# First rows of the q and k stacks loaded from ScalarE's queue, and one value projection moved behind the third attention block

## The reference, cut to what matters

```python
qkv = (xw @ h_qkv_w)                      # window branch: q_w, k_w, v_w
attn = softmax(einsum('bghnd,bghmd->bghnm', q, k) * SCALE)
q = (xh.reshape(B, H * W, C) @ l_q_w)     # pooled branch: 1024 queries
pooled = xh.reshape(B, hg, WS, wg, WS, C).mean(axis=(2, 4)).reshape(B, G, C)
kv = (pooled @ l_kv_w)                    # 256 keys and values
attn = softmax(einsum('bnhd,bmhd->bhnm', q, k) * SCALE)
x = x + attention(_gn(x))
x = x + conv3x3(relu(_gn(x) * mask(_gn(x)))) + bias
```

## Time and profile before

| what | value |
|---|---|
| runs | 347.93, 349.73, 350.08 us (median 349.73) |
| span of the profiled execution | 347.5 us, from its first to its last instruction |
| TensorE busy | 315.2 us |
| VectorE / ScalarE / GpSimd busy | 272.5 / 148.8 / 83.0 us |

### The profile page before, as it was taken

One profiled execution on the slowest core, in us unless ns is written; L12 is line 12 of the kernel. 1 busy time (PEld: TensorE's weight loads), 2 busy tenths in 40 slices (PEclk: granted clock), 3 DMA queues, 4 the chain that ended last, 5 costly groups with the idle time before them and its releaser, 6 DMA issues.

```text
span 347.5 us, 4162 instructions
## 1 busy us (share of the span) xinstructions
PE 315.2 (91%) x1566; PEld 222.3 (64%) x1566; DVE 272.5 (78%) x488; ACT 148.8 (43%) x189; POOL 83.0 (24%) x46
## 2 busy tenths in 40 slices
PE   0879968999979999999799999999799999999995
PEld 0566344267866663688567744888388727877884
DVE  4996668769999586889989767799887847897572
ACT  2442548464490843554047855351165423031300
POOL 2088513440436020003910200008600200202000
PEclk9999968899989999999999999999999999999999
DMA  8779500009700000099011200197001000101002
GB/s 276 276 102 140 228 5 0 2 1 134 94 0 4 2 1 2 0 130 159 1 63 41 82 1 2 35 128 128 4 0 62 0 0 5 58 0 62 0 0 121
DMA packets 12068, 20.38 MB, mean 59 GB/s; under 512 B 2065, under 2 KB 8081, under 8 KB 11793
## 3 DMA queue, kind: packets, MB, share of 16 engines
q1 hardware_dynamic: 12048, 20.13, 28.2%
HBM read 7.93 MB, written 4.19 MB: 35 GB/s over the span
## 4 chain that ended last, share of the span: by engine, by line
PE 58%; DVE 23%; ACT 8%; issue 6%; POOL 3%; DMA 2%; SPq 0%; DVEq 0%; POOLq 0%
PE slot L1113 29%; PE cps L1145 15%; PE slot L1189 7%; DVE l_max L848 3%; PE cps L1113 3%; DVE mask L784 3%; PE cps L1189 2%; ACT probs L563 2%; POOL probs L379 2%; DVE v_lo L814 1%; DMA xy<-x 1%; PE slot L1392 1%; ACT xn_hi L452 1%; ACT p_w L608 1%; DVE xn L740 1%
## 5 line engine op out<-in xcount | busy, mean ns | idle before, releaser
L1145 PE MATMUL cps<-v_hi,cw_hi 128*128 128x512 f32 (+1 forms) x144 | 57.6, 400 | 3.5 <-DVE v_lo L814 2.9
L1145 PE MATMUL cps<-v_hi,cw_lo 128*128 128x512 f32 (+1 forms) x144 | 57.9, 402 | 0.0
L1145 PE MATMUL cps<-v_lo,cw_hi 128*128 128x512 f32 (+1 forms) x144 | 56.4, 392 | 0.0
L379 POOL TENSOR_TENSOR probs<-q_w,k_w 128x1024 f32<-128x1024 f32 x14 | 32.9, 2376 | 79.5 <-DVE rw L777 72.3
L848 DVE TENSOR_REDUCE l_max<-slot 128x4 f32<-128x1024 f32 x32 | 37.1, 1216 | 5.9 <-PE slot L1113 5.9
L563 ACT ACTIVATE probs<-slot 128x1024 f32<-128x1024 f32 x32 | 31.4, 1021 | 16.0 <-PE slot L1113 15.9
L1145 PEld LDWEIGHTS cps<-v_hi,cw_hi 128*128 128x128 f32 x144 | 27.4, 191 | 12.7 <-issue 5.2
L1145 PEld LDWEIGHTS cps<-v_hi,cw_lo 128*128 128x128 f32 x144 | 27.4, 190 | 7.4 <-issue 2.2
L1145 PEld LDWEIGHTS cps<-v_lo,cw_hi 128*128 128x128 f32 x144 | 27.4, 190 | 5.0
L362 POOL TENSOR_TENSOR mask<-rw 128x1024 f32<-128x1024 f32 x8 | 15.2, 1912 | 56.6 <-DVE rw L777 56.6
L1113 PE MATMUL slot<-xn_hi,w_hi 128*128 128x512 f32 (+1 forms) x68 | 27.3, 401 | 1.1 <-ACT xn_hi L452 1.1
(11 more groups left out here) (197 smaller groups left out, 635.0 us busy)
## 6 DMA issues: line engine op xcount, KB each, us to landing
xy<-x SPq DMA_DIRECT2D x8, 512.0 KB, 6.6
out<-xy SPq DMA_DIRECT2D x8, 512.0 KB, 2.6
qs<-probs SPq DMA_DIRECT2D x12, 256.0 KB, 5.8
qs<-probs SPq DMA_DIRECT2D x24, 128.0 KB, 8.3
raw_cw<-conv_w SPq DMA_DIRECT2D x2, 1152.0 KB, 6.4
ks<-probs SPq DMA_DIRECT2D x12, 128.0 KB, 6.9
probs<-h_qkv SPq DMA_DIRECT2D x2, 192.0 KB, 3.8
probs<-l_kv SPq DMA_DIRECT2D x2, 128.0 KB, 3.7
```

Source lines behind the costliest of these rows:

```text
L379: nc.gpsimd.tensor_tensor(product(b, j).rearrange("p (n w) -> p n w", n=NW), q_w[:].rearrange("p (n w) -> p n w", n=NW), k_w[:, j * G:(j + ...
L1145: ins = nc.tensor.matmul(cps[:, pos % 2, y0 * WT:y1 * WT], (cw_hi, cw_hi, cw_lo)[part][:, k, pos, dy + 1, o * P:(o + 1) * P], (v_hi, v_lo, ...
```

## The change

Of the twelve transfers of `stack(b)`, the four that write rows 0 to 31 move from SP's list to ScalarE's. The first half of q_hi is issued behind the copy `lq_hi`; k_hi and the two late quarters of q_hi are issued one after the other behind the copy `lk_hi`, ahead of `values_of`. Ahead of each of the two places ScalarE waits for its own copy to be complete. Destinations, sizes and semaphore counts are the same. In image 0 the projection of v_w goes from ahead of the attention blocks to behind block 2.

```diff
@@ stack(b), SP
                 sp.wait_ge(lq_act, b + 1)
-                queries(0, lq_hi, slice(0, HALF), stacked)
                 queries(2, lq_hi, slice(0, HALF), stacked)
                 sp.wait_ge(lq_dve, b + 1)
                 queries(1, lq_lo, slice(0, HALF), stacked)
                 sp.wait_ge(lk_act, b * 2 + 1)
-                keys(0, lk_hi)
                 keys(1, lk_hi)
                 sp.wait_ge(lk_dve, b + 1)
                 keys(2, lk_lo)
                 for quarter, done in zip((2, 3), stacked_late):
-                    for part, parts in enumerate((lq_hi, lq_lo, lq_hi)):
+                    for part, parts in ((1, lq_lo), (2, lq_hi)):
                         queries(part, parts, slice(quarter * G, (quarter + 1) * G), done)
@@ ScalarE
+            def own_queries(n, done):
+                act.dma_start(qs[0:HD, :, n].bitcast(F32), lq_hi[:, n].bitcast(F32)).then_inc(done, 16)
+            def own_keys():
+                act.dma_start(ks[0:HD].bitcast(F32), lk_hi.bitcast(F32)).then_inc(stacked, 16)
@@ projections(b, first), ScalarE
                 nc.scalar.copy(lq_hi, flat[0]).then_inc(lq_act, 1)
+                act.wait_ge(lq_act, b + 1)
+                own_queries(slice(0, HALF), stacked)
                 if b == 1:
                     sum_moments(0, 1, probs[:, 3])
...
                 nc.scalar.copy(lk_hi, slot[1][:, 0, 0:G]).then_inc(lk_act, 1)
-
+                act.wait_ge(lk_act, b * 2 + 1)
+                own_keys()
+                for quarter, done in zip((2, 3), stacked_late):
+                    own_queries(slice(quarter * G, (quarter + 1) * G), done)
                 if b != 1:
                     values_of(slot[1])
@@ front(b, conv, first), TensorE
                     project(slot[1], WV)
-                else:
-                    project(cps, WV)
                 conv.more(fill[1])
...
                     else:
+                        if first and n == 3:
+                            project(cps, WV)
                         pe.wait_ge(la_max, b * NB + n - 2)
```

## The result

The changed kernel takes 359.42 us (355.81 to 360.97, 4 runs), beside 348.92 us (347.93 to 350.08, 4 runs) for the one before. The ratio on record is 1.0265, with a 95% interval of 1.0219 to 1.0311; the two medians alone give 1.030. The profiled executions span 357.0 and 347.5 us, so 9.5 us are to be found in the traces. Every run's time on record is 2.2 to 2.3 us more than its span.

The account below looks back on a forecast made before the run. It took TensorE as busiest, but led by other engines in the images' fronts. Image 0 2.6, image 1 1.0, images 2 and 3 3.9 sum to 7.5 us: span 347.5 to 355.0, plus 2.2 gives 357.2 us (352.5 to 362).

Parts of the forecast that it names:

- rival 2: All stack transfers: two queues move no more bytes than one (137 GB/s), `stacked` at 31.8, sum 9.3, 359.0 us; chance 0.26.
- the forecast's own: Whole kernel: the band of 355.3 to 358.1 us around the forecast of 357.2 us, chance 0.40.
- An issue on ScalarE costs 0.6 us of its list: ScalarE's four issues an image: 0.6 us each, as on SP; three behind `lk_hi` with the copy's wait +1.95 us.
- Rival 1: ScalarE's issues are nearly free, 0.1 us each, so the whole takes 354.2 us; chance 0.15.
- Images 2 and 3 pay it in full: Images 2 and 3: `values_of`, `key_lo`, `row_sums` and the products hang in a row, 1.95 us longer in each, 3.9 us.
- the shadow: Images 2 and 3: TensorE's means wait for the later q_w copy, up to 1.8 us, hidden behind VectorE's 1.95 us.
- Image 1 pays 1.0 us: Image 1: stack 1.0 us later, beside 0.7 us from the first issue; the larger counts, +1.0 (bounds 0.7 and 1.9).
- the prediction's bound at 137 GB/s: Image 1's stack: at 137 GB/s instead of the 150 taken, it lands 1.9 us later.
- The stack in image 0 is late by its bytes: Image 0: 1.44 MB rather than 1.18 move before `stacked` is full; at 150 GB/s that is at 30.9 us.
- The value projection costs what the stack leaves uncovered: Image 0: the moved projection no longer fills TensorE's wait for `stacked`; window scores start later, +2.6 us.
- `stacked` + 5.55: Image 0: start of the window scores, after three blocks (1.69), the projection (2.80) and the v_w copy (1.06).
- Rival 3: Not slower: two queues reach 200 GB/s and issues cost under 0.3 us; 349 to 352.5 us, chance 0.13.

## Why the prediction was right, point by point

The forecast was 357.2 us with 352.5 to 362; it is 359.4. Of the 9.5 us in the traces the sum had 7.5. The time lies in the band given to rival 2 (358.1 to 362), not in the forecast's own, and rival 2's condition, block 0 at 31.8, holds. But its sum of 9.3 us came near 9.5 partly by luck: it has 1.9 us for image 1, where 0.03 was paid, and nothing for the clock. The 2.2 us from the span to the median was taken over as a difference of this case; the runs show it as nearly the same in every execution. By its steps:

**An issue on ScalarE costs 0.6 us of its list.** Right: 0.58, 0.86 and 0.64 in a row. One of three was longer, and with the wait for the copy `values_of` starts 2.3 us later against the marks around it, not 1.95. Rival 1 (0.1 us an issue) is out: one issue ahead of `values_of` costs image 2 0.78 us, three cost 2.3.

**Images 2 and 3 pay it in full.** Right in mechanism, +2.32 and +2.36 for 1.95 each. With `values_of` put first the `row_sums` distance from image 1 to image 2 is 72.44 for 72.40. The prediction took these chains for VectorE's and called TensorE's lateness a shadow; both proved true, and the turned order showed the shadow to be worth 0.4 to 0.5.

**Image 1 pays 1.0 us.** Wrong: +0.03, and by two errors. The first is in the stack, which was to land 1.0 us later behind 0.26 MB more. The changed kernel's timeline in image 1, SP's queue, ScalarE's queue and TensorE:

```profile
84.90 1.20 SPq L279 DMA_DIRECT2D ks<-probs  x2
85.52 1.53 ACTq L503 DMA_DIRECT2D qs<-probs  x2
...
93.47 0.64 PE L1124 MATMUL slot<-ks,qs 96*128 96x256 f32 x4
```

`key_lo` does not wait for `values_of` in image 1, so SP issues both its k parts at once, the second at 85.54, beside ScalarE's first late quarter. Its semaphore tells of the landing at 93.02, 11.27 us behind `query_lo` (before 11.21), and block 0 does not wait for it. The bytes that the prediction counted ahead of k_lo are not ahead of it here. Where they are, with the late quarters issued first on SP's queue, the same block waits 2.10 us and comes 1.9 later, which is the prediction's bound at 137 GB/s.

The second error is in the first issue. Its delay is there: the means of image 0 start at 84.76, 3.01 us behind `query_lo` (before 2.19), and block 0 stands 11.72 behind it (before 11.25; with the first issue alone 11.71). What failed is the reading of the earlier trace rows as the chain that binds. That chain before the change has more rows than were read, two of them with no releaser:

```profile
88.54 0.87 issue
89.41 2.38 ACT xn L532 x2
91.85 1.07 issue
```

Two stretches of 0.87 and 1.07 us called issue, in a chain that jumps from engine to engine, can be room that a late step uses up; that the 0.82 us of the first issue cost nothing says that here they were. VectorE's own timeline before says who led:

```profile
89.42 0.20 DVE L777 TENSOR_SCALAR rw<-rw 128x64 f32<-128x64 f32 x1
89.53 2.35 DVE L848 TENSOR_REDUCE l_max<-slot 128x4 f32<-128x1024 f32 x2
```

From `query_lo` to these maxima VectorE's timeline shows no wait for another engine, so VectorE led here and TensorE's block had some 0.2 us of room. In the changed kernel block 0 is 0.47 later and the maxima only 0.27 (94.14 less 81.75, for 89.53 less 77.41), and the masked image starts 0.53 later. That too is absorbed, by the masked image itself. The two rows are of the kernel before and of the changed one, and give ns min/median/max:

```profile
L784 DVE SCALAR_TENSOR_TENSOR mask<-mask,xn x2: 1211/1512/1814, 92.9 to 94.7; 128x1024 f32<-128x1024 f32 x2
```

```profile
L795 DVE SCALAR_TENSOR_TENSOR mask<-mask,xn x2: 1211/1256/1300, 97.8 to 99.0; 128x1024 f32<-128x1024 f32 x2
```

Before, the first of the two took 1.81 us, as it started at 92.92 while GpSimd's mask sums ran to 93.65; now it starts at 97.79, with those sums done at about 98.0, and takes 1.30. `v_lo` behind it starts 20.9 us from `query_lo` in both. That GpSimd's traffic stretched it is an inference from the two timelines; the lengths are measured.

**The stack in image 0 is late by its bytes.** Right, and mis-sized. The prediction put 150 GB/s in the middle between 137 and 168; the changed kernel has 135 and 136 GB/s from 28 to 32 us, and block 0 at 31.75, where rival 2 said 31.8 and the forecast 30.9. That was 0.9 us of the sum. The 168 of the earlier trace rows was measured with SP's queue alone, so no row showed that a second queue raised it. The Trainium skill has this in DMA: Bandwidth & Descriptors, Issuing engines are not separate DMA queues: whichever engine issues them, transfers end on the same 16 DMA engines. The trace agrees, with 31.73 for one queue and 31.75 for two. The same section calls the saved sequencer time small; here it was SP's time, which nobody waited for, that was saved, and ScalarE's 0.6 us an issue that was spent.

**The value projection costs what the stack leaves uncovered.** Right: `stacked` + 5.55 was the structure, and the move alone gives 5.56. Missing was the clock. The prediction wrote down that TensorE would stand idle from 27.2 until the stack is full, and priced the matmuls behind the gap at the durations of the earlier trace rows, that is at 2.4 GHz. They ran at 1.2 GHz until about 36: 5.55 became 7.50 (39.25 less 31.75). This is the largest term that the sum lacks, +1.9. The fall goes with a wait of TensorE and not with the move as such: with the late quarters ahead on SP's queue and the projection in its old place, 11.54 us from block 0 to the last maxima became 13.47 behind a gap of 1.85 us, and with `values_of` first there was no fall behind 2.73 us.

Image 0 thus had +5.37 (stack 1.80, move 1.63, clock 1.94) for a forecast of 2.6. Of this 1.03 us is missing again at image 1's start, and that is no merit of the change. From the last maxima of image 0 to `query_lo` of image 1 it takes 35.92 us before, 34.89 in the changed kernel, and 34.80 to 34.96 in nine of the ten variants with a trace, three of them without any issue on ScalarE. Stretches of the kernel before and of the changed one, columns as above:

```profile
46.00:50.00 4.00, 2.78 (x9) 2.31 (x10) 3.38 (x8) 1.80 (x3) 0.00 (x0) 0.55 0.03 6
50.00:54.00 4.00, 3.75 (x13) 2.72 (x12) 1.73 (x3) 2.55 (x4) 2.75 (x2) 0.59 0.00 0
```

```profile
50.00:54.00 4.00, 2.26 (x13) 1.62 (x11) 2.49 (x8) 0.86 (x2) 0.00 (x0) 0.89 0.04 10
```

The kernel before had the low clock for some 7 us from 46 on in its profiled execution, the changed one only for some 3 us from 53 on. The tenth variant, with the late quarters back on SP, has it for some 7 us from 52 on, and there the stretch takes 36.08 us. So the 1.03 us go with the length of this fall.

**The end.** +0.45 us behind image 3's maxima was in no step. There the changed kernel has a fall of the clock at 254 to 258 us (granted 0.57 in that stretch, 1.00 before). Others have it too, three of them variants of the kernel before, with 112.2 to 112.3 us behind image 3's maxima, so it can't be put down to the edit.

So the total came near by a sum of errors that partly cancel: the time up to image 1 1.7 us too low, images 2 and 3 0.8 too low, the end 0.45, and image 1 1.0 too high. Rival 3 (not slower) is out on both its conditions. What stays open is how much of the clock's 1.9 us a median run has: falls come and go from run to run, and only one execution of each kernel has a trace.

## What to carry to other kernels

A transfer's issue is some 0.6 us of the list it stands in, and moving it from a queue that nobody waits for to an engine on the chain of every stage costs that much each time; if it must be there, put it behind the step that others wait for. While the DMA engines are full, what is issued ahead of the transfer that releases work decides when that one lands, and a second queue changes nothing. When work that fills a wait of TensorE is moved away, price the gap twice: its length, and, as a risk and not a certainty, the matmuls behind it at the lower clock.

## What the runs showed of the hardware

- **Two queues, one rate, nearly one order.** Parts of 128 KB issued at 21.9, 22.5, 23.4 (ScalarE) and 24.95 us (SP) landed at 28.8, 29.8, 30.7 and 31.7 in the changed kernel, in the order of issue and 0.95 us apart: 138 GB/s for both queues together. With all of them on SP's queue the last four landed at the same times to 0.03 us. The order is not strict between queues: where SP's issue began 0.02 to 0.13 us behind ScalarE's first late quarter (image 1 of the changed kernel, images 0 to 2 with `values_of` first), SP's landed first, by some 0.95 us.
- **The length of a gap does not settle whether the clock falls.** Around idle time of 4.63 us on TensorE the granted clock was 0.50 for some 6 us, and it fell around gaps of 3.04 us (`row_sums` first), 2.86 (late quarters back on SP) and 1.85 (late quarters ahead on SP). Around one of 2.73 us (`values_of` first) it did not. In several kernels, with the change and without it, the first projections ran at the lower clock at 19 to 28 us in the profiled execution: 42 matmuls took 11.05 us there instead of 7.91, in the version with seven idle rounds for instance and not in that with ten, which is the same program up to there. The Trainium skill says as much (TensorE: Matmul & The Clock Gate, Part 1: The HAM clock gate (the "warmup" mystery)): how many matmuls a kernel runs at the lower clock at its start differs between its own runs. The traces agree, and show it in mid-kernel too. The times go with it: of 56 runs of the kernel before that were taken beside the variants, those with a mean granted clock of 0.984 or 0.985 took 347.5 to 350.3 us, those with 0.966 or less 352.6 to 354.1.
